# The two tiled layouts of the matrix engine trade places inside each pair of attention heads

## What is computed

```
x = x + xattn0(layernorm(x), ctx)   # 16 heads of 64; q, k, v, softmax over 375 context rows, Wo
x = x + ffn0(layernorm(x))          # shared + two routed experts, 256 -> 1024 -> 256, relu
x = x + xattn1(layernorm(x), ctx)   # one head of 256, masked rows
x = x + ffn1(layernorm(x))          # int8 quantised 256x256
```

```
q = xn @ Wq; k = ctx @ Wk; v = ctx @ Wv
sim = q k^T / 8;  attn = softmax(sim);  out = attn @ v;  x += concat(out) @ Wo + bo
```

## Time and profile before

| | |
|---|---|
| median of three runs | 1028.74 us (1027.96 to 1029.76) |
| the profiled execution | 1028.21 us |
| its span, first to last instruction | 1026.4 us |
| outside the span | 1.8 us |
| granted TensorE clock, mean | 0.983 of full |
| busy: PE, DVE, ACT, POOL | 95%, 60%, 49%, 23% |
| end of the first attention block (last `mix_pair`) | about 686 us |

### The profile page before, as it was taken

One profiled execution on the slowest core, in us unless ns is written; L12 is line 12 of the kernel. 1 busy time (PEld: TensorE's weight loads), 2 busy tenths in 40 slices (PEclk: granted clock), 3 DMA queues, 4 the chain that ended last, 5 costly groups with the idle time before them and its releaser, 6 DMA issues.

```text
span 1026.4 us, 20038 instructions
## 1 busy us (share of the span) xinstructions
PE 979.3 (95%) x6876; PEld 827.7 (81%) x6876; DVE 614.2 (60%) x1606; ACT 502.1 (49%) x1198; POOL 233.4 (23%) x296
## 2 busy tenths in 40 slices
PE   5999999999999999999999999989999999999764
PEld 4878888888888888888888888868988888898733
DVE  6865456555565555645655556569665565664567
ACT  4665555555555555555555555544324324234233
POOL 0323333332332333333333333220000000000204
PEclk9999999999999999999999999999999999999985
DMA  9200000000000000000000000003401201202102
GB/s 296 83 2 17 0 15 15 0 15 0 15 15 0 15 15 0 15 0 15 15 0 15 7 8 0 2 32 142 119 2 42 79 0 45 74 1 73 48 1 72
DMA packets 20077, 33.63 MB, mean 33 GB/s; under 512 B 1616, under 2 KB 16496, under 8 KB 19040
## 3 DMA queue, kind: packets, MB, share of 16 engines
q1 hardware_dynamic: 20048, 33.25, 10.6%
HBM read 31.41 MB, written 1.84 MB: 32 GB/s over the span
## 4 chain that ended last, share of the span: by engine, by line
PE 91%; DVE 5%; ACT 2%; issue 1%; DMA 0%; POOL 0%; DVEq 0%; ACTq 0%
PE bank L1222 27%; PE bank L1374 11%; PE bank L1440 11%; PE bank L1263 9%; PE bank L1236 8%; PE bank L1243 8%; PE bank L1204 6%; PE bank L1284 4%; PE bank L1403 2%; PE bank L1423 2%; ACT probs L546 1%; PE bank L1192 1%; PE bank L1411 1%; PE bank L1387 1%; DMA x_all<-in_x 0%
## 5 line engine op out<-in xcount | busy, mean ns | idle before, releaser
L458 POOL TENSOR_TENSOR probs<-probs,row_rcp 112x375 f32<-112x375 f32 x256 | 202.6, 813 | 456.0 <-DVE row_rcp L791 456.0
L786 DVE TENSOR_REDUCE neg_max<-bank 112x1 f32<-112x375 f32 x256 | 128.3, 543 | 125.0 <-PE bank L1236 125.0
L546 ACT ACTIVATE probs<-bank,neg_max 112x375 f32<-112x375 f32 x256 | 144.7, 571 | 95.0 <-DVE neg_max L786 95.0
L647 ACT ACTIVATE hid<-bank,b_col 128x448 f32<-128x448 f32 x96 | 61.0, 635 | 160.4 <-PE bank L1440 158.1
L1263 PE MATMUL bank<-probs_t,v 125*64 125x112 f32 x1536 | 101.9, 267 | 3.6 <-DVE probs_t L796 2.8
L1243 PE MATMUL bank<-ident,probs 112*125 112x112 f32 x768 | 104.0, 271 | 0.0
L1263 PEld LDWEIGHTS bank<-probs_t,v 125*64 125x64 f32 x1536 | 74.6, 136 | 36.4 <-issue 32.0
L1243 PEld LDWEIGHTS bank<-ident,probs 112*125 112x125 f32 x768 | 98.8, 188 | 4.0 <-issue 0.4
L1236 PE MATMUL bank<-k_parts,q_parts 64*112 64x376 f32 x768 | 98.0, 360 | 2.2 <-ACT probs L546 2.2
L1222 PE MATMUL bank<-ctx_hi,wk_hi 128*128 128x376 f32 x256 | 97.5, 381 | 0.8 <-DVE q_parts L776 0.6
L1008 DVE CAST hid_hi<-hid 128x448 fp32r<-128x448 f32 x96 | 37.7, 393 | 100.2 <-ACT hid L647 99.3
(11 more groups left out here) (150 smaller groups left out, 1984.9 us busy)
## 6 DMA issues: line engine op xcount, KB each, us to landing
ctx_raw<-in_ctx_t SPq DMA_DIRECT2D x16, 375.0 KB, 3.4
stage<-in_ffn_up SPq DMA_DIRECT2D x3, 1024.0 KB, 4.8
stage<-in_ffn_down SPq DMA_DIRECT2D x3, 1024.0 KB, 6.8
stage<-in_ctx_t SPq DMA_DIRECT2D x8, 375.0 KB, 4.9
stage<-in_ctx_n SPq DMA_DIRECT2D x8, 375.0 KB
ring_more<-in_ctx_t SPq DMA_DIRECT2D x8, 375.0 KB, 6.5
ring_more<-in_ctx_n SPq DMA_DIRECT2D x8, 375.0 KB
x_all<-in_x SPq DMA_DIRECT2D x1, 1344.0 KB, 14.6
```

The source lines that it names most:

```text
L458: eng.tensor_tensor(probs[r][:, :], probs[r][:, :], row_rcp[:, r:r + 1].broadcast_to([S, C]), ALU.mult).then_inc(probs_ready, 1)
L546: eng.activation(probs[r][:, :], bank[2 + r % 2][0:S, 0:C], ACT.Exp, bias=neg_max[:, r:r + 1], accum_out=row_sum[:, r:r + 1]).then_inc(exp ...
L786: eng.tensor_reduce(neg_max[:, r:r + 1], bank[2 + r % 2][0:S, 0:C], AX.X, ALU.max, negate=True) \
```

## The change

`mix_pair` and `pair_scores` trade places in each step of the batch loop on the matrix engine. Nothing else is changed: no instruction, no wait and no other engine's list.

```diff
@@ -1297,13 +1297,13 @@
                 for c, u, project, bf in halves(b, last):
                     for s in range(0, HH, 2):
                         g, n = HH * u + s, HH * c + s
-                        pair_scores(g, u, c, s)
                         if not (first and n < 4):
                             back = s < 4
 
 
                             turned = (B if last else b + 2) if c == 1 else b - 1
                             mix_pair(u - 1 if back else u, (1 - c) if back else c, (s - 4) % HH, turned)
+                        pair_scores(g, u, c, s)
                         if last and c == 1 and s == 2:
                             eng.wait_ge(gate_step, 4)
                             eng.wait_ge(proj_used[1], unit_count(u, 7))
```

## The result

The changed kernel takes 1068.37 us, the median of four runs (1067.66 to 1069.04), against 1029.24 us for the kernel before on the same chip: a ratio of 1.0382, with a 95% interval of 1.0364 to 1.0400. The forecast was 1061 with a range of 1050 to 1071. Direction and mechanism came out as forecast; the loss is 39 us, where the sum said 33. The measured time lies just above the 1055 to 1067 that the prediction gave its forecast by itself, and inside the stated range.

A forecast was written before the change was run, and what follows sets the result against it. The prediction took PE, busy 95% of the span, to bound the kernel. Losses of 26.0 + 4.0 + 2.8 = 32.8 us on the profiled 1028.2 gave 1061.0, stated as 1061, range 1050 to 1071.

The forecast's parts named there:

- the sum: Whole kernel: 26.0 us in 28 repeating halves, 4.0 in the beginning, 2.8 in the last half, 32.8 us in all.
- The array keeps its price: PE, each step: three layout changes removed and three added cost the same; start to first unit stays 1.42 us.
- s = 0 to s = 2: Batch loop: products of s = 2 wait for DVE's copy and start at 216.01, not 215.93, losing 0.08 us.
- s = 2 to s = 4: Batch loop: the scores-to-copy chain moves by 0.72; period 5.18 us, PE waits 0.85 ahead of the products of s = 4.
- Steps s = 4 and s = 6: Batch loop: no wait in either, with cover of 0.93 us in s = 4 and over 1 us in s = 6.
- The thin cover of bank 1: k units into bank 1 wait for the last unit's low part; cover 0.86 us, 0.09 left, so no loss.
- The beginning: First 86 us: 1.9 for two ordinary losses, 1.4 at two half beginnings, 0.7 for the first wait; 4.0 us.
- The first wait: In the beginning, at 31 to 36 us: the first wait of all, counted at 0.7 us.
- ordinary loss: A half with units and products in all steps loses 0.08 + 0.85 = 0.93 us; two lie in the beginning.
- the two beginnings of halves: In the first 86 us: products already wait for a copy; scores now come behind that wait, 0.70 us each.
- The last half: No units there: the scores of four steps come out from under existing waits, 0.70 each, 2.8 us.
- An array that pays for columns before rows: Rival: columns to rows costs one exit more (0.09 us) in 126 steps, 11 us on top, 1072; chance 0.07.

The follow-up runs named there:

- e1: Against the kernel before, products first in steps s = 0 and s = 6 only: 1034.05 us against 1027.98, ratio 1.0059.
- e6: The changed kernel with `mix_pair`'s waits, except the two for the copies, put ahead of the transposes of s = 2: 1062.83 us, ratio 1.0331.
- e4: The changed kernel with both copies of the transposed probabilities in s = 2 moved one place up: 1037.30 us, ratio 1.0085.
- e10: The changed kernel with copies of s = 2 one place up, long-met waits moved away, scores first in the last half: 1033.07 us against 1028.19.

## Why the prediction was right, point by point

- *The array keeps its price.* Right. Products to scores 0.72 to 0.73 us, scores to a whole block 0.70, and from a whole block to the products as long as it was to the scores (the transposes of `xn` to the next block: 0.28 us, 90.02 to 90.30, and 85.84 to 86.12 before). TensorEngine Tiling (Array Packing) in the Trainium skill, section Key Properties, says that a change of tiling mode drains the engine. The trace agrees so far as a change costs something (0.26 us where 0.17 is the pace) and three changes a step cost the same in either order; the drain itself no run shows. e1, with the new order in s = 0 and s = 6, bounds the difference at 0.02 us a changed step.
- *s = 0 to s = 2.* Forecast 5.17, measured 5.17 to 5.18. DVE's copy hangs on the q unit, which kept its place.
- *s = 2 to s = 4.* The mechanism was right, the term too small: forecast 5.18, measured 5.25 and 5.40. The term that was mis-sized is the hand-over. I took 0.05 us from the one pair of rows at 680.32. The other wait in that same group of rows, at 676.28, has 0.25 us between DVE's copy (done at 676.03) and the products. It is the same `mix_pair` with s = 0 and c = 1 that stands in step s = 4, with the same waits in front, while the pair at 680.32 is a `mix_pair` with the copies' waits alone, like the one of step s = 2, where 0.05 came true. A mean of 0.175 instead of 0.05 is 3.5 us over 28 halves. The loop missed 4.1 (30.1 for 26.0); the other 0.6 are the 0.02 us by which the chain was longer than read (4.43 for 4.41).
- *Steps s = 4 and s = 6.* No wait, as forecast (6.11 and 5.25 us).
- *The thin cover of bank 1* held: no wait of L1222 in the loop.
- *The beginning*: 4.0 forecast, 4.2 measured, the closeness in part by luck. The first wait (0.7), the first ordinary loss (1.0 for 0.93) and the two beginnings of halves (0.77 and 0.89 for 0.70 each) are there. The second ordinary loss is only 0.7, and 0.26 us came in a step that the sum left at nothing (31.97 to 36.93, before 31.42 to 36.12).
- *The last half*: 2.8 forecast, 5.0 measured. The term was about right for the waits: in e6, where the clock fell only at the end of this half, it takes 21.5 us, 3.2 more than before, and 0.6 of those are its last products at half clock (1.32 us where 0.73 is the block), which leaves 2.7. That is the sum and not its parts: the forecast had 0.70 in each of four steps, while there from products to products two steps grew by 1.3 and two by 0.3 to 0.4, and the first products began 0.70 earlier. The other 2 us or so, and the 1.1 in the feed-forward part, are the clock, which the sum had at nothing: I wrote that it would be granted in full over the attention block, and it was, up to the last half. I gave no reason for leaving it out.
- *The rivals.* An array that pays for columns before rows would have fitted the total (1072) better than my own sum did. The stated range reached to 1071 because of that rival, and the measured 1068.37 lies above the 1067 of the forecast by itself; that the range held is owed to the room left for an effect that did not occur. Only the timeline, e1 and the two runs with repairs, e4 and e10, tell that the total came from elsewhere.

## What to carry to other kernels

Before two blocks on one engine trade places, ask for each what it waits for and what it releases. Moving the block that waits forward and the block that releases back shortens one semaphore loop from both ends, here by 0.70 and 0.72 us against a cover of 0.50 and 0.35 in turn, and a swap that costs nothing on its own engine costs 4%. Two swaps that each lean on the same cover don't add up, so test them together.

When a wait becomes the bound, the instructions that stand between it and the first useful one count too: put waits for things long done elsewhere, out of the way of the one that comes last.

## What the runs showed of the hardware

- A wait that holds several semaphores is several instructions of PE's sequencer, some 0.1 us from one to the next. With them the first matmul starts 0.10 or 0.25 us behind the end of DVE's copy, and 0.05 with only the copies' own waits left (e6).
- Whatever layout comes next, a block takes the same time within 0.02 us: the scores, in rows, 0.69 to 0.70 us ahead of columns and 0.70 to 0.71 ahead of the whole array; the products, in columns, 0.72 to 0.73 ahead of either.
- In the changed kernel the granted clock went to its lower level (1.2 GHz) 1.3 us after a wait of PE of 1.74 us, while it stayed full through 28 halves with one wait of 0.85 or 1.00 us each. In e6 it stayed full after a wait of 1.73 us. After the fall four matmuls took 3.35 us instead of 1.77.
